# One relu ahead of the decay and the carry copy in ScalarE's order within a tick

## What is computed

```python
# layer 0, each image
y = leaky_relu(conv2d_3x3(x, conv_w1, conv_b1))
y = leaky_relu(conv2d_3x3(y, conv_w2, conv_b2))
seq = y as (4096, 64)
# a selective state space model over the 4096 positions, 128 channels x 16 states
h = exp(d_t * A) * h + (d_t * u_t) * b_t        # one step of the scan
y_t = sum over states of h * c_t
out = (y + x * D) * silu(z) @ out_proj_w
# layer 1, each image
out_c = softmax(xc xc^T) x                      # attention over channels, 64 x 64
out_s = v softmax(q^T k)^T                      # attention over positions, 4096 x 4096
x = x + w_bn [out_c; out_s]
```

## Time and profile before

| | |
|---|---|
| median of 3 runs | 9698.47 us (9694.0 to 9716.83) |
| the profiled execution, its time | 9699.92 us |
| its span, first to last instruction | 9698.1 us |
| TensorE busy | 8341.3 us, 86% |
| VectorE busy | 7451.8 us, 77% |
| ScalarE busy | 6341.1 us, 65% |
| GpSimd busy | 3263.7 us, 34% |
| mean granted TensorE clock | 0.954 of full speed |

### The profile page before, as it was taken

How to read it: one execution, slowest core, us unless ns; L and a number is a source line. 1 busy time by engine, 2 the same in 40 slices (tenths; PEclk the granted TensorE clock), 3 DMA queues, 4 the chain that set the end, 5 groups by cost and what they waited for, 6 DMA issues and landing times. The chain is left out here.

```text
span 9698.1 us, 136670 instructions
## 1 busy us (share of the span) xinstructions
PE 8341.3 (86%) x38979; PEld 2211.9 (23%) x39622; DVE 7451.8 (77%) x11112; ACT 6341.1 (65%) x12445; POOL 3263.7 (34%) x2315
## 2 busy tenths in 40 slices
PE   8884349898989898998989898989989898989999
PEld 2221012222222222222222222222222222222222
DVE  1115988888888888888888888888888888988632
ACT  1113457776767777776767777777777776777654
POOL 0003544333333333333333333333434333433200
PEclk9996569999999999999999999999999999999999
DMA  6455876666667676667667676767666666667400
GB/s 91 81 92 139 207 191 168 169 171 168 174 161 181 156 184 162 179 168 174 169 168 176 160 179 163 180 163 182 170 171 171 167 170 170 175 162 179 117 21 8
DMA packets 799817, 1512.11 MB, mean 156 GB/s; under 512 B 347752, under 2 KB 381232, under 8 KB 799024
## 3 DMA queue, kind: packets, MB, share of 16 engines
q1 hardware_dynamic: 795952, 1502.62, 63.3%
q10 hardware_dynamic: 3072, 0.40, 0.0%
HBM read 1309.36 MB, written 176.16 MB: 153 GB/s over the span
## 5 line engine op out<-in xcount | busy, mean ns | idle before, releaser
L1189 POOL TENSOR_TENSOR hst<-hst,cbc 128x512 f32<-128x512 f32 x2048 | 2849.0, 1392 | 5005.8 <-ACT carry L959 4223.5
L948 ACT ACTIVATE pr<-bank 128x512 f32<-128x512 f32 x4096 | 2230.9, 596 | 1181.2 <-PE bank L831 1167.2
L1089 DVE TENSOR_TENSOR_SCAN hst<-dA,carry,bank 128x512 f32<-128x512 f32 x1792 | 2293.9, 1280 | 67.0 <-ACT dA L954 2.9
L840 PE MATMUL bank<-pr,vt 128*64 128x512 f32 x8192 | 2245.2, 627 | 0.0
L1034 DVE CUSTOM_DVE_ANT_0 gains<-bank,gains 128x512 f32<-128x512 f32 x2048 | 1391.0, 687 | 894.3 <-ACT gains L894 867.9
L1081 DVE TENSOR_TENSOR bank<-lanes,bbc 128x512 f32<-128x512 f32 x2048 | 1699.2, 830 | 191.5 <-issue 119.5
L829 PE MATMUL bank<-s1q,s1k 128*128 128x512 bf16 x3453 | 1336.1, 387 | 550.9 <-DMA t2q<-nm 168.4
L954 ACT ACTIVATE dA<-lanes,small 128x512 f32<-128x512 f32 x2048 | 1486.4, 726 | 278.2 <-DMA lanes<-spread_d 179.5
L831 PE MATMUL bank<-t2q,t2k 128*128 128x512 bf16 x4096 | 1568.7, 383 | 87.7 <-issue 43.5
L894 ACT ACTIVATE gains<-bank 128x512 f32<-128x512 f32 x2048 | 1225.1, 601 | 501.8 <-PE bank L777 469.1
L777 PE MATMUL bank<-s1kx,s1q 128*128 128x512 bf16 x4096 | 1298.5, 388 | 188.4 <-DVE mxp L1034 137.2
(11 more groups left out here) (110 smaller groups left out, 6398.8 us busy)
## 6 DMA issues: line engine op xcount, KB each, us to landing
lanes<-spread_d SPq DMA_DIRECT2D x2048, 512.0 KB, 5.0
seqt<-seq_d SPq DMA_DIRECT2D x256, 128.0 KB, 4.5
spread_d<-dsp SPq DMA_DIRECT2D x128, 256.0 KB, 2.0
spread_d<-usp SPq DMA_DIRECT2D x128, 256.0 KB, 2.0
bbc<-bc_d SPq DMA_DIRECT2D x128, 256.0 KB, 3.4
cbc<-bc_d SPq DMA_DIRECT2D x128, 256.0 KB, 3.9
xpad<-in_x SPq DMA_DIRECT2D x64, 256.0 KB, 6.6
ypad<-ypad SPq DMA_DIRECT2D x128, 128.0 KB, 2.8
```

The source lines that it names most:

```text
L840: mm = nc.tensor.matmul(ACC[CH * h:CH * (h + 1), :], vt[:, t, :], pr[:, T % PRING, h, :], start=t == 0, stop=t == KT - 1)
L948: nc.scalar.activation(pr[:, T % PRING, h, :], bank_of(("S", T, h))[:], ACT.Exp).then_inc(S["p_full"], 1)
L1089: nc.vector.tensor_tensor_scan(hst[:, T % HRING, :], dA[:, T % 2, :], DBU[:], carry[:, g:g + 1] if sl else 0.0, ALU.mult, ALU.add).then_in ...
L1189: nc.gpsimd.tensor_tensor(h, h, cbc[:, (T - 1) // GROUPS % 2, :], ALU.mult).then_inc(S["hc_in"], 1)
```

## The change

ScalarE asks for the tick's list of small uses right behind the exponentials. If the first is a search difference, its relu comes at once, ahead of the decay and the carry copy; what is left of the list stays where it was. In ticks with two search differences the second relu stays behind. No other engine's order is touched, and nothing is added or left out.

```diff
@@ ScalarE, in the loop over ticks, behind the two exponentials
+                        ev = sched.small_uses(T)
+                        near = 2 if ev and ev[0][0] == "dif" else 0
+                        for e in ev[0:near]:
+                            small_use(e)
                         if sched.spreads(T + 1):
                             wait(act, f"lanes{(T + 1) % SLOTS}", T + 1, 16)
                             wait(act, "scan", T - 1)
...
                             nc.scalar.copy(carry[:, g:g + 1],
                                            hst[:, (T - 1) % HRING, CHUNK - 1:CHUNK]).then_inc(S["carried"], 1)
-                        for e in sched.small_uses(T):
+                        for e in ev[near:]:
                             small_use(e)
```

## The result

The changed kernel takes 9821.73 us (median of 5 runs, 9809.58 to 9839.97) for 9698.47: 1.0123 times the time, interval 1.0108 to 1.0139, which is 123 us slower. The forecast was 9775 in a range of 9630 to 9850. The sign is right and the time lies in the range; the sum is 47 us short.

The account below looks back on a forecast made before the run. Bound by handovers between nearly full TensorE and VectorE. Terms 3.6 + 0.8 - 1.2 + 2.1 = 5.3 us a step, times 14.5 = 77 us, giving 9775 us from the median 9698.5; range 9630 to 9850.

Parts of the forecast that it names:

- ScalarE's rival: Cover for what stands behind the waiting relu on ScalarE fails once in each of 8 slices: +157 us, 9855; chance 0.13.
- The engine that sets the end: Main loop: TensorE and VectorE nearly full, neither full alone; the end is set by what they hand to each other.
- the port: VectorE instructions with two SBUF inputs and GpSimd's SBUF reads shut each other out; VectorE's DBU (product into a bank) ends 0.56 after GpSimd.
- Most ticks give nothing: Where TensorE has only just made the scores, the relu already starts 0.48 behind its product and can't come sooner.
- Place A: Ticks 25, 57, 89, 121: VectorE's rest finds GpSimd's usp running and ends 0.9 later, four times, 3.6 us a step.
- B: Ticks 9, 41, 73, 105: relu 0.69 sooner, but VectorE's rest meets usp and ends 0.2 later, four times, 0.8 us.
- D: Ticks 52, 84, 116: GpSimd's multiply gets ahead of VectorE's DBU; +0.7 between 0 and 1.2, three times, 2.1 us.
- Place C: Ticks 1, 33, 65, 97: VectorE gains 0.69 and TensorE 0.31; value -0.3, four times, -1.2 us a step.
- ticks 17 to 22: The fourth stretch of its kind: stretches VectorE has now would go and others come, put at 0.
- TensorE's clock stays: Sign for the changed profile: the second max of a pair and TensorE's clock stay as before.
- The signs: VectorE's relu wait falls from 231 to some 180 us; relu's product wait +240; L1081 and rest lengthen; exponentials wait less.
- The faster one: Rival: VectorE gets in first, A and D 0, B -0.69, C -0.3: -58 us, 9641; chance 0.27.

Follow-up runs that it names:

- only_BC: The change in ticks 1 and 9 of each 32 alone, against the kernel before: 9746.35 us, ratio 1.0044.
- but_17_22: The change everywhere but in ticks 17 to 22 of a step, which keep the old order, against the kernel before: 9776.93 us, ratio 1.0076.
- late_carry: Kernel before with the first relu between dA, which keeps its place, and the carry copy, so only the carry goes behind it: 9806.44 us, ratio 1.0091.
- short_after: The changed kernel with GpSimd multiplying only 8 of 512 columns: 9471.54 us, ratio 0.9751 against the kernel before.
- short_before: The kernel before with GpSimd multiplying only 8 of 512 columns: 9530.57 us, ratio 0.9815 against the kernel before.
- only_A: The change in ticks 24 and 25 of each 32 alone, against the kernel before: 9759.30 us, ratio 1.0058.
- only_D: The change in ticks 19, 20 and 21 of each 32 alone, beyond tick 32, against the kernel before: 9760.60 us, ratio 1.0047.
- picked_9_10_25: Kernel before with the order carry copy, early relu, dA in ticks 1, 9, 10 and 25 of each 32: 9665.46 us, ratio 0.9948.
- early_carry: Kernel before with ScalarE's order exponentials, carry copy, first relu, dA, the rest: 9766.67 us, ratio 1.0054.
- picked: Kernel before with the order carry copy, early relu, dA in ticks 1 and 9 of each 32 alone: 9670.18 us, ratio 0.9964.

## Why the forecast was right, and where it was short

**The time.** 9821.73 lies in the range, but 47 us from the forecast and 33 from the 9855 of ScalarE's rival, which is itself above the range's 9850 that was said to reach it. The time alone does not choose between the two; the experiments do.

**The engine that sets the end, and the port.** Right. VectorE is busy longer with fewer instructions, by DBU and rest, and with the multiply cut to 8 columns the same reordering gains 59 us. The 0.56 that VectorE ends behind GpSimd is there in each collision shown (0.55, 0.55, 0.56).

**Most ticks give nothing.** Right for TensorE and VectorE's waits: the relu starts as its product ends, and the list by ticks is 0 in most.

**Place A.** Right in mechanism and in size (0.84 for 0.9). It is worth 2.5 and not 3.6, because the last slice has no carry copy to move. **B** and **D** right: 1.0 for 0.8, 2.0 for 2.1.

**Place C.** -1.5 for -1.2 where it arises, but `only_BC` has it returned in the next tick. "Both run on nearly full" was not enough to keep a gain; the forecast needed to follow C one tick further. What takes the gain back there was not traced.

**The term that was mis-sized: ticks 17 to 22.** "Stretches that VectorE has now would go and others come: 0" had no row behind it. It measured +2.3 a step in the list, and 46 to 54 us by `but_17_22`, about the 47 that the forecast is short. That the rest comes to +69 for the forecast's +77 is in part luck: A is 1.1 a step less than forecast, and ticks 5, 6 and 67, put at nothing, are 1.9 more. I had balanced collisions by count; what counted was that one of them (ysb right behind the multiply, on DBU) delays a max for which TensorE then idles 2.59 us.

**"TensorE's clock stays."** Wrong: at tick 22 the granted clock is 0.67 in the window where it was 1.00, and in steps 3 to 13 of after it falls also at tick 41 three times and at tick 105 seven times, where before has no fall. At tick 22 no run separates clock and collision for the change itself. In `late_carry`, where the clock falls there in 8 of 11 steps, ticks 21 to 23 take 14.8 us without a fall and 15.5 with one, for 14.2 before.

**The signs.** VectorE's wait for the relu fell to 158, below the 180 forecast; the relu's wait for its product rose by 173, not 240; both means rose. The exponentials wait less, as forecast.

**The rivals.** The faster one needs VectorE to win its races; it lost each by the 0.07 to 0.26 us worked out, and with the races taken away a number close to its own appears. ScalarE's: `short_after` keeps every wait behind the relu and is faster than `short_before`, and `late_carry`, with dA in its old place, has most of the loss; so it falls as an addition to the forecast's mechanism. Its cover failed only to the +0.6 to +0.7 of ticks 24, 56, 88 and 120 that the forecast already had.

**The quarter changes.** At ticks 47 and 48, 79 and 80, 111 and 112, where a quarter of the step changes, `only_A` is 1.9 us a step longer than before, `only_BC` 1.2, `only_D` 2.8 and `picked_9_10_25` 2.4, whether the kernel gains or loses elsewhere; `early_carry`, which loses much inside the quarters, is 4.1 shorter there, ticks 46, 78 and 110 with them. TensorE waits there for the maxima that come by DMA; its waits for that transfer over the run are nearly the same in before (168 us on matmuls, 235 on weight loads) and in `picked_9_10_25` (172, 238), and shorter in `early_carry` (119, 189).

What the traces show beside it is TensorE's clock. Ticks 79 and 80 of before in two steps, as windows:

```profile
5250.66:5259.32 8.66, 6.48 (x36) 1.43 (x32) 7.46 (x7) 5.31 (x12) 2.53 (x2) 1.00 0.99 233
5780.48:5790.97 10.49, 8.08 (x36) 1.74 (x32) 7.43 (x7) 5.36 (x12) 2.53 (x2) 0.84 0.90 209
```

The same 36 matmuls take 1.60 us longer where the clock falls. Of the 33 quarter changes in steps 3 to 13 it falls at 11 in before and in `picked`, at 17 in `only_BC`, 21 in `only_A` and after, 22 in `picked_9_10_25`, 26 in `only_D` and at none in `early_carry`. The three ticks around a quarter change take some 12.9 us in before without a fall and 14.5 with one. So most of what the three single places lose there goes with more frequent falls, and less than half of what `early_carry` gains.

**Open.** Why the clock falls oftener at quarter changes in one kernel than in the other is not shown. TensorE's longest idle time there does not tell: in before it is 2.1 to 2.6 us with a fall and 1.8 to 2.8 without. The +1.1 of ticks 5 and 6 wasn't taken apart either.

## What to carry to other kernels

When an instruction is moved within an engine's order, the first question is which engine it starts: here a copy of one column, moved by 0.5 to 1.3 us, sent a 1.27 us GpSimd instruction upon VectorE's, and cost more than the removed wait gave. Lay the started instruction, and the one queued behind it, over the other engine's timeline in each different tick, and give no such tick a zero by balance: the ticks that got one held about what the forecast was short of. Where the wait to be removed stands in few places, move the order in those places alone (9665 us beside a before of 9710, where the change has 9822 beside 9698), and measure, since of the gains that were expected only half reached the end. When a stall of TensorE grows, look at its granted clock in every step, not in one: in `early_carry` it fell in some steps and not in others, and a fall cost 1.6 us beside 1.26 for the collisions.

## What the runs showed of the hardware

A VectorE product of two 128x512 operands in SBUF takes 0.69 us alone and 0.94 to 1.81 in the rows where GpSimd got in first, ending 0.55 to 0.57 after it; the 64x768 rest goes from 0.95 to 1.83. It is not only GpSimd's length that matters: in `early_carry` DBU kept 826 ns and the loss came by rest and other instructions of VectorE. The max with one operand in a bank kept its mean of 687 ns in before and in after.

All of GpSimd's long multiplies together cost the kernel before 184 us (9714.43 - 9530.57), clock included (at the 33 quarter changes it falls 11 times in before and never in `short_before`), though GpSimd is busy only a third of the span and mostly waits for the carry copy.

TensorE's clock fell to its lower level in some steps and not in others. In tick 22, after 2.59 us of idle time, the granted clock in the window of 10.4 us was 0.67, and products took 0.61 for 0.39 us; after 1.34 us in the same tick of before it stayed at 1.00. In ticks 26 to 28 of `early_carry` it stayed at 1.00 with an idle time of 2.71 us in one step and fell with 2.70 in the next. A fall cost 1.60 us of matmul time there, and 1.60 at a quarter change of before: more than the 1.26 that the collisions in ticks 26 to 28 cost.
